# Chebyshev layer of a graph network: the products of two terms, not one, are made beside the third gather

## What is computed

```python
def _cheb(x, prop, w, b):
    Tx0 = x
    out = Tx0 @ w[0]
    if K > 1:
        Tx1 = prop(Tx0)
        out = out + Tx1 @ w[1]
        for k in range(2, K):
            Tx2 = 2.0 * prop(Tx1) - Tx0
            out = out + Tx2 @ w[k]
            Tx0, Tx1 = (Tx1, Tx2)
    return out + b
def prop(h):
    return jax.ops.segment_sum(wn[:, None] * h[row], col, num_segments=n)
feats = [_cheb(x, prop, w2, b2), _cheb(x, prop, w3, b3), _cheb(x, prop, w4, b4)]
concat = jnp.concatenate(feats, axis=1)
scale_w = jax.nn.softmax(concat @ attn_w + attn_b, axis=1)
fused = jnp.concatenate([feats[i] * scale_w[:, i:i + 1] for i in range(3)], axis=1)
h = fused @ fus_w + fus_b
```

## Time and profile before

| | us |
|---|---|
| median of three runs | 14526.22 (14521.36 to 14529.68) |
| the profiled execution, time | 14521.27 |
| its span in the trace | 14519.6 |
| third gather's stage, first gather to last bridge | 10562 to about 11084 |
| slots' stage | 11099 to about 11700 |

### The profile page before, as it was taken

The page is one execution under the profiler, slowest core; times in us unless marked ns, Lnnn a source line. Parts: engine busy times, 40 slices in busy tenths (PEclk is TensorE's granted clock), DMA queues, the critical chain, the costliest instruction groups (busy, mean ns, idle before and its releaser), DMA issues. The chain is left out here.

```text
span 14519.6 us, 105608 instructions
## 1 busy us (share of the span) xinstructions
PE 5141.8 (35%) x25061; PEld 4156.3 (29%) x25061; DVE 8613.3 (59%) x14550; ACT 3939.6 (27%) x10228; POOL 8127.0 (56%) x8280
## 2 busy tenths in 40 slices
PE   0000002000000001200005444576767977888876
PEld 0000002000000001100005334455546976666554
DVE  8870345444444445522477678776755778568865
ACT  0000011000000001100262342266644257654431
POOL 0557777777777777777407750177763000640767
PEclk9955555555555555555555555587878965899555
DMA  6200234433433444411375433344466667777753
GB/s 218 112 5 1 52 90 138 118 114 113 118 114 113 118 114 122 129 54 54 125 239 161 129 118 108 108 140 131 137 208 225 229 239 272 244 252 242 224 168 110
DMA packets 955385, 2071.04 MB, mean 143 GB/s; under 512 B 318121, under 2 KB 323519, under 8 KB 938640
## 3 DMA queue, kind: packets, MB, share of 16 engines
q1 hardware_dynamic: 689040, 1702.87, 34.3%
q0 software_dynamic: 265728, 361.43, 11.1%
HBM read 1251.36 MB, written 822.13 MB: 143 GB/s over the span
## 5 line engine op out<-in xcount | busy, mean ns | idle before, releaser
L731 POOL DMA_INDIRECT hop_raw<-hop_table,i_hop x2352 | 2219.5, 944 | 734.3 <-issue 686.3
L527 POOL DMA_INDIRECT gine_raw<-x,i_near x392 | 376.2, 960 | 1433.4 <-POOLq L89 1314.2
L755 DVE TENSOR_TENSOR hop_rows<-hop_raw,hop_factors 128x672 f32<-128x672 f32 x336 | 289.8, 863 | 1494.4 <-DMA hop_raw<-hop_table,i_hop 1494.4
L825 PE MATMUL hop_rows<-hop_chain,src_carries 128*128 128x96 f32 x12 | 4.3, 450 | 3023.6 <-DVE hop_chain L801 3023.6
L833 ACT ACTIVATE hop_keeps<-src_inner 128x672 f32<-128x672 f32 x336 | 255.4, 762 | 2664.9 <-DVE hop_chain L801 2613.0
L527 POOL DMA_INDIRECT cheb_raw<-cheb_table,i_cheb x784 | 817.0, 1042 | 245.1 <-issue 236.5
L825 PEld LDWEIGHTS hop_rows<-hop_chain,src_carries 128*128 128x128 f32 x12 | 3.0, 311 | 3024.9 <-issue 3024.9
L527 POOL DMA_INDIRECT cheb_raw<-x,i_near x392 | 447.0, 1140 | 647.8 <-POOLq L89 528.6
L527 POOL DMA_INDIRECT gine_raw<-conv,i_near x392 | 395.7, 1009 | 603.4 <-POOLq L89 484.2
L1803 POOL DMA_INDIRECT own_raw<-x,i_dst x392 | 388.2, 990 | 594.7 <-POOLq L89 475.6
L1594 PE MATMUL cheb_base_product<-folded,cheb_base_turned_rows 97*128 97x292 f32 x1568 | 561.8, 514 | 180.0 <-ACT cheb_base_mixed L1553 180.0
(11 more groups left out here) (538 smaller groups left out, 21337.1 us busy)
## 6 DMA issues: line engine op xcount, KB each, us to landing
hop_res<-hop_table SPq DMA_DIRECT2D x336, 336.0 KB
hop_table<-hop_sums SPq DMA_DIRECT2D x336, 336.0 KB
part<-cheb_put_mixed SPq DMA_DIRECT2D x49, 1168.0 KB
cheb_slots_ends_part<-part SPq DMA_DIRECT2D x49, 1168.0 KB
start_x_x<-x_and_map SPq DMA_DIRECT2D x98, 400.0 KB, 3.7
x<-start_x_rows SPq DMA_DIRECT2D x98, 400.0 KB
cheb_base_term<-x SPq DMA_DIRECT2D x98, 400.0 KB
mid<-cheb_base_rows SPq DMA_DIRECT2D x98, 400.0 KB, 4.5
```

What stands on the lines that cost most here:

```text
L527: pool.indirect_dma_start(out=raw_rows[:, b % RAW, g, :], out_offset=None, in_=table, in_offset=bass.IndirectOffsetOnAxis(ap=index[:, t:t ...
L731: pool.indirect_dma_start(out=raw_rows[:, b % RAW, g, :], out_offset=None, in_=table, in_offset=bass.IndirectOffsetOnAxis(ap=index[:, t:t ...
L755: nc.vector.tensor_tensor(by_channel(b).rearrange("p c t -> p t c"), raw[:, b % RAW, :, :], spread(weights[:, at], C), ALU.mult).then_inc( ...
L825: nc.tensor.matmul(carried, side.carries[:, :], chain[:, (batches - 1) % LINES, :, EDGE - 1], start=True, stop=True).then_inc(s["carried"], 1)
```

## The change

The job beside the third gather gets a second source, the term of power 1 (`cheb_a`), whose transposed rows ScalarE copies; its products are accumulated onto those of power 0 in the same 292 columns before they are stored to `part`. The slots' stage has two sources instead of three, powers 2 and 3. Since these reach only the columns 96 to 291, its addition covers 196 columns instead of 292 (`low`). The load of `cheb_a`, 49 transfers of 128 x 768 values (384 KB), moves from the slots' stage to the third gather's. The sizes of `part` and of its store and load stay.

```diff
@@ class ChebRows, __init__ @@
         self.side = side
+        self.low = min(self.from_column(power) for _, _, power in self.sources)
         self.narrow = part_in is not None
@@ class ChebRows, vector @@
             for c in range(4):
-                into = self.mixed[:, i % self.DEPTH, q % 2 * 4 + c, :]
+                into = self.mixed[:, i % self.DEPTH, q % 2 * 4 + c, self.low:MIX]
                 dve.wait_ge(self.sem(ph, "product"), 4 * q + c + 1)
-                self.nc.vector.tensor_tensor(into, into, self.product[c][:, 0:MIX], ALU.add)\
+                self.nc.vector.tensor_tensor(into, into, self.product[c][:, self.low:MIX], ALU.add)\
                     .then_inc(self.sem(ph, "taken"), 1)
@@ graph_layers @@
         propagate("cheb3", cheb_c, cheb_b, k.i_cheb,
-                  (ChebRows(nc, k, "put", False, slots, [(0, x2_slots)], part, part_out=True, turns=2, copies=("dve",)),))
-        sources = [(1, cheb_a), (2, cheb_b), (3, cheb_c)]
+                  (ChebRows(nc, k, "put", False, slots, [(0, x2_slots), (1, cheb_a)], part, part_out=True, turns=2,
+                            copies=("dve", "act")),))
+        sources = [(2, cheb_b), (3, cheb_c)]
         slot_rows(nc, k, "cheb_slots", ChebRows(nc, k, "ends", False, slots, sources, mid_slots, part_in=part,
-                                                gram=(total, False), turns=2, side=by_dst, copies=("act", "act", "act")))
+                                                gram=(total, False), turns=2, side=by_dst, copies=("act", "act")))
```

## The result

The changed kernel takes 14457.7 us (median of 5 runs, 14455.8 to 14467.9), the kernel before 14526.2 beside it on the same chip (14521.4 to 14533.3): a ratio of 0.9954, interval 0.9940 to 0.9969. The profiled execution spans 14461.3 us, against 14519.6.

What follows compares the result with a forecast made beforehand. TensorE bounds the slots' stage, a ring of engines the third gather's. 14521.3 less 112 (slots), plus 40 (gather), less 1 (first batch landing sooner) gives 14448 us profiled, 14453 as a median; range 14408 to 14510.

Steps and rivals of the forecast that it cites:

- the ring: Third gather's stage: TensorE's second step, ScalarE's group 2 and sums, VectorE's chain and copy set the pace; 8.73 to 10.6 us.
- The gather's stage, +40: Third gather's stage: 47 blocks with two steps go from 9.75 to 10.6 us at full clock, 40 us more.
- The slots' stage, -112: Slots' stage: 49 batches go from 12.21 to 9.9 us, 112 us less, bounds 138 and 10.
- The walk of the batch at full clock: Slots' stage: 3.5 us from first addition to mix, plus 5.85 to the next batch, a period of 9.4 us.
- the 0.55 us on top of it: Slots' stage: TensorE's clock falls in a third of the batches, some 1.7 us each time, 0.55 on the mean.
- The forecast's line between the rests of 2.47 and 2.74 us: TensorE's clock: fell after a 2.47 us rest, held after 2.74; a 1.9 us rest put where it holds.
- The loads, "nothing": Slots' stage: the load of 384 KB per batch that goes was costed at nothing, DMA share 0.65 to 0.69.
- A: Rival, slots' stage: the clock holds through the rests, 9.4 us a batch, 138 us saved, 14427 us; chance 0.18.
- B: Rival, slots' stage: the clock swings with every batch, near 11.6 us, 30 us saved, 14535 us; chance 0.09.
- C: Rival, third gather's stage: the ring with the clock down at 0.54, 360 us more instead of 40, 14773 us; chance 0.07.
- D: Rival, gather's ring: a new wait for the second load or ScalarE's copy, 1 us a block, +47, 14500 us; chance 0.09.
- The sum: Whole kernel: 14521.3 - 112 + 40 - 1 = 14448 us for the profiled execution, 14453 for a median.

Runs made afterwards that it cites:

- b_early: The kernel before, with ScalarE taking groups 0 and 1 and VectorE 2 and 3 beside the third gather: 14521.7 us, ratio 0.9990.
- g_early: The changed kernel, with ScalarE taking groups 0 and 1 and VectorE 2 and 3 beside the third gather: 14435.5 us, ratio 0.9928.
- s_noadd: The changed kernel without the last addition of VectorE's mix, so one part is missing from the slots' rows: 14323.9 us, ratio 0.9853.
- s_deep: The changed kernel with 5 buffers instead of 4 in the slots' stage and loads issued three batches ahead instead of two: 14471.8 us, ratio 0.9955.
- sd_fill: The changed kernel with eight unread transposes in TensorE's rest, 5 buffers and loads three batches ahead in the slots' stage: 14431.8 us, ratio 0.9934.
- s_fill: The changed kernel with eight unread transposes per batch in TensorE's rest ahead of the odd step's products, slots' stage: 14472.0 us, ratio 0.9950.

## Why the prediction was right, and where its sizes were off

- **What bounds each stage** held: TensorE in the slots' stage before, the ring in the gather's stage. b_early moved the ring by the product that the forecast's sum had in it; g_early moved it as far as TensorE's own work allows.
- **The gather's stage, +40:** measured +35.2. The ring's 10.6 us came as 10.71 and the clock as 0.98. The mean of before was too low, worked out as 9.75 from estimated ends of the stage: between the last sums of blocks with two steps it is 9.99 in the trace. The mean after is 10.74, also above the forecast's 10.6, and so part of that error cancels: each block grew by 0.75 instead of 0.85 us.
- **The slots' stage, -112:** measured -93.9. The walk of the batch at full clock held (9.46 for 9.4; s_noadd shows its bound). The term that failed is the 0.55 us on top of it. It took the clock to fall in a third of the batches at 1.7 us each. The price of a fall is right (1.66), the frequency is too low: the clock fell in 20 of 48 batches, in after as in s_deep, and not in 16. The forecast's line between the rests of 2.47 and 2.74 us had no ground: the same 1.73 us is followed by either clock.
- **The loads, "nothing":** wrong as an argument. The share of DMA came out as forecast (0.68 for 0.69), but it says nothing of when a load lands. The load is issued once a batch, and TensorE asked for it sooner after its issue (7.8 us) than it landed (9.8). Clock and landing together cost 41.4 us (sd_fill), where the forecast had 0.5 x 49 = 24.5. That difference of 17 us is nearly the whole miss of 18 in this stage. By an estimate from the intervals, 20 falls of 1.66 us are 33 of the 41; the rest is falls that lasted longer (batches of 12.03) and landings that came later still (up to 13.35). The landing's own share can't be had from a single edit, since VectorE's rest takes its place.
- **The rivals.** A, the clock holds, is what sd_fill had to be built for. B, a fall in every batch, came in 20 of 48. C did not come: the gather's clock is at 0.98. D, a wait in the gather's ring for the second load or copy, has no row.
- **The sum.** Of 14 us between -73 and -58.7, 18 are the slots' stage, and 5 go the other way in the gather's. The forecast for the profiled execution was thus 15 us too low (14448 for 14463.0). That the median came nearer, 14457.7 for 14453, is luck: it lies 5 us below the profiled execution this time and lay 5 above it before.

## What to carry to other kernels

Work moved from a full engine into a ring where that engine idled can cost less than its length, if its clock had been falling there (here 35 us for 98 steps with 2.36 us of work more each): read the granted clock of both stages, and look whether the engine would rest now in the one that loses the work. When an engine stops being the bound, ask two things of each rest: does its clock survive, and was a load issued early enough for the shorter period, which a DMA share does not tell. Where two causes can fill the same idle time, removing either one may show nothing; a run with both removed belongs to the plan from the start.

## What the runs showed of the hardware

- The granted clock fell behind 18 of 38 rests of 1.73 us in s_deep, and held behind the other 20. With 0.86 us of rest it stayed at 1.00 (sd_fill). A fall cost 1.66 us 15 times, and 2.56 three times.
- Transposes that nothing reads paid for themselves: eight per batch 39.3 us where the deeper load was in place (sd_fill against s_deep), twelve per step in the gather's stage of before 22.4 us. Without the deeper load the eight showed nothing clear (s_fill).
- A batch's loads of 1936 KB were ready 9.8 us after their issue, beside 225 GB/s in the window, where TensorE asked after 7.8.
- An addition of 196 columns out of TensorE's results took 0.357 us, one of 292 0.456.
